# Constant matmuls on TensorE around the last norm of the first layer's batches, in a two-layer decoder kernel

## The chip, the cores and the metric

The kernel runs on one core of a Trainium2 chip, in one launch. The metric is the device time of that launch in microseconds. Engines are called by the profile's names: PE is TensorE's matmul, PEld its weight load, DVE is VectorE, ACT is ScalarE, POOL is GpSimd, and SP is SyncE, which only issues DMAs here.

## The reference, cut to what matters

The whole is a decoder of two layers on x of shape (4, 512, 256) in float32; each sublayer is added to the stream after a layer norm.

```python
x = x + _L0_attn_ref(_layernorm(x), ...)            # selective scan, then attention and a gated FFN
x = x + _L0_xattn_ref(_layernorm(x), ctx_1024, mask, ...)
x = x + _L0_ffn_ref(_layernorm(x), ...)             # 8 experts, top 1
x = x + _L1_attn_ref(_layernorm(x), ...)
x = x + _L1_xattn_ref(_layernorm(x), ctx_1024, ctx_1024, ...)
x = x + _L1_ffn_ref(_layernorm(x), ...)             # 16 experts, top C tokens, and a shared FFN

def _layernorm(x, axis=-1, eps=1e-05):
    m = jnp.mean(x, axis=axis, keepdims=True)
    v = jnp.var(x, axis=axis, keepdims=True)
    return (x - m) / jnp.sqrt(v + eps)

def step(h, inp):                                    # the selective scan, 512 steps, 512 channels, 16 states
    x_t, d_t, B_t, C_t = inp
    dA = jnp.exp(d_t[:, :, None] * A)
    h = dA * h + d_t[:, :, None] * B_t[:, None, :] * x_t[:, :, None]
    y_t = jnp.sum(h * C_t[:, None, :], axis=-1)
    return (h, y_t)
```

The change lies in the norm before the first layer's expert FFN, and reaches into the start of the next batch's scan.

## The kernel before, in words

The program is written out by hand: each engine has its own instruction stream, and semaphores order them. Activations are kept with features on the partitions, 2 x 128 features by the 512 tokens of one batch (`xb`, `xc`, `sq`, `xn`). PSUM has 8 banks of 512 float32 columns.

After a first part that computes the scan's inputs for all four batches comes the loop of L743, `for b in range(B)`, once per batch:

1. **The scan** (L795 to L809). For each of the 16 states PE makes the input term: `input_term(n)` (L774) multiplies four 128x128 blocks of `duT` for each of four channel groups with diagonal blocks that ACT wrote (`spread_b`, L1525, seen as L1530), into banks 4 to 7. DVE scans each bank against the decays that ACT exponentiated (L1523; the scans are L1963). POOL multiplies the scanned states with C (L2462), and PE adds the product to y (`add_to_y`, L787, seen as L791). `input_term(n + 2)` stands before the addition of state n, so PE's order is input term, addition, input term, addition.
2. The output projection (L815), attention, the gated FFN, and cross-attention, whose last product goes through L967 into banks 2 and 3. DVE adds it to `xb` (L1958).
3. **The end of the batch** (L971 to L988), where the change lies. PE makes the mean in bank 0 (two matmuls of 512 columns, seen as L642, which is the line of the helper `acc`). If there is a next batch, PE then makes that batch's first input term, `input_term(0, b + 1)`. DVE centres (L1806), ACT squares (L1431). `norm_var(3, 1)` puts the variance in bank 1, eight matmuls with one moving column each. ACT takes the root (L1435), DVE inverts it (L1810), and `norm_rows(3, 0)` spreads the factors over the 128 partitions in bank 0, four matmuls of 128 columns, seen as L660. DVE multiplies (L1815, `xn`). PE transposes `xn` (L983) into the tiles of group "xn" for ACT (L1638), which stores it for the routing, and makes the router's logits, matmuls of 8 columns (L642 again), in bank 3. DVE adds their bias (L2079).

DVE's stream at the end of a batch, in order: L1806, L1810, L1815, the scans of channel groups 0 and 1 of the next batch's state 0, the logits' addition (L2079), then the scans of groups 2 and 3 and on into the next batch's loop. ACT's stream there: squares, `spread_b(1)`, the root, the decays of state 0, the two drains of the transposes (L1638), then the loop of the next batch.

PE's next instructions after the logits are `input_term(1)` and `input_term(2)` of the next batch. `input_term(n)` waits, for each of the four channel groups, for the scan of that group in state n-1 (L781), since it overwrites its bank. After the fourth batch the routing of the expert FFN follows instead: it needs the logits on DVE, and PE has two small matmuls in it (L994, L995).

A float32 matmul appears in the trace as two records with two weight loads; a transpose appears as one record.

Of the kernel before, what the change touches and what calls it, by code (L numbers as in the profile page):

```python
# [6 lines left out]
B, L, D = 4, 512, 256  # L7
# [130 lines left out]
def decoder_program(nc, A, out):  # L138
# [5 lines left out]
    with ctx:  # L144
# [17 lines left out]
        def take(*shape, at=None):  # L162
            n = int(np.prod(shape))
            o = top[0] if at is None else at
            if at is None:
                top[0] += n
                assert top[0] <= WORDS, top[0]
            v = arena[:, o:o + n]
            if len(shape) == 2:
                v = v.rearrange("p (a b) -> p a b", a=shape[0])  # L170
            if len(shape) == 3:
                v = v.rearrange("p (a b c) -> p a b c", a=shape[0], b=shape[1])
            return v
# [15 lines left out]
        const = take(C_COLS)  # L189
        vec = take(V_COLS)  # L190
        ident = const[:, C_ID:C_ID + P]
# [155 lines left out]
        bank = [psum[:, i, :] for i in range(8)]  # L347
# [288 lines left out]
        def _(pe):  # L636
            mm, transpose = nc.tensor.matmul, nc.tensor.transpose

            def acc(dst, pairs):

                for i, (w, x) in enumerate(pairs):
                    r = mm(dst, w, x, start=i == 0, stop=i == len(pairs) - 1)  # L642
                return r
# [47 lines left out]
            for s in range(B + 2):  # L691
# [34 lines left out]
                if b1 < B:  # L726
                    for half, f, n in ((0, a_r0, 1), (1, a_r1, 5)):
# [3 lines left out]
                        for c in range(NC):  # L731
                            r = mm(bank[4 + half][:, c * P:(c + 1) * P], f[:, c:c + 1].broadcast_to([P, P]), ident,
                                   start=True, stop=True)
# [9 lines left out]
            for b in range(B):  # L743
                def w(s, n):
                    pe.wait_ge(s.sem, s.at(n, b))
# [28 lines left out]
                def input_term(n, b=b):  # L774

                    pe.wait_ge(diag_ready.sem, diag_ready.at(NC * (n + 1), b))
                    for c in range(KI):
                        if n == 0:
                            pe.wait_ge(ld_scan.sem, ld_scan.at(48, b))
                        else:  # L780
                            pe.wait_ge(scan_done.sem, scan_done.at(KI * (n - 1) + c + 1, b))  # L781
                        for q in range(NC):
                            r = mm(bank[4 + c][:, q * P:(q + 1) * P], duT[:, q, c * P:(c + 1) * P], diag[n % 2][:, q, :],  # L783
                                   start=True, stop=True)
                        r.then_inc(b_full.sem, 1)
# [186 lines left out]
                norm_mean(xb, 0)  # L972
                if b + 1 < B:
                    input_term(0, b + 1)
                norm_var(3, 1)
                norm_rows(3, 0)
                w(na.out, 4)
                for half in range(2):
                    t = LA.fill(pe, b, "xn", half)
# [47 lines left out]
            def w0(s, n):  # L1027
                pe.wait_ge(s.sem, s.at(n))
# [15 lines left out]
            def norm_var(i, squares, at):  # L1044
                w0(nb.sq, KD * (i + 1))
                for c in range(NC):
                    r = acc(bank[at][:, c:c + 1], [(squares[:, k, c * P:(c + 1) * P], mean1[:, 0:1]) for k in range(KD)])
                r.then_inc(nb.var.sem, 1)

            def norm_rows(i, factors, at):  # L1050
                w0(nb.rs, i + 1)
                for c in range(NC):
                    r = mm(bank[at][:, c * P:(c + 1) * P], factors[:, c:c + 1].broadcast_to([P, P]), ident, start=True, stop=True)
                r.then_inc(nb.rows.sem, 1)
# [343 lines left out]
            for n in range(E1):  # L1398
# [14 lines left out]
                for hf in range(2):  # L1413
                    for k in range(KH):
                        if hf == 0 and k >= KH - 3:
                            pe.wait_ge(he_ready.sem, he_ready.at(k + 1, n))
                        r = mm(bank[6 + hf][:, 0:D], h1[:, k, hf * P:(hf + 1) * P], wdb[j][:, k, :],  # L1417
                               start=k == 0, stop=k == KH - 1)
# [1224 lines left out]
```

## Time and profile before

| | |
|---|---|
| median of 3 runs | 2991.7 us |
| lowest, highest | 2984.35, 3001.02 us |
| the profiled execution's own time | 2999.19 us |
| its span, first to last instruction | 2997.4 us |
| mean granted clock of TensorE in it | 0.933 of full |
| PE busy | 2666.6 us (89%) |
| DVE, ACT, POOL busy | 1454.4, 1087.9, 682.0 us |

The span is what the trace shows from its first to its last instruction; 1.8 us of the execution's time lie outside it. An engine's busy time says how long it had work in flight, not that it set the pace: that is read stretch by stretch, from what ended its idle time. The granted clock is given as a fraction, 1.00 for 2.4 GHz and 0.50 for 1.2 GHz.

### The profile page before, as it was taken

The numbers are of one execution on the slowest core, as the hardware profiler recorded it, in microseconds if no ns is written. First come the engines' busy times: TensorE is split into PE (matmuls) and PEld (weight loads), VectorE is DVE, ScalarE is ACT, GpSimd is POOL, SyncE is SP. The second block draws the span as 40 slices with busy tenths as digits, with TensorE's granted clock in tenths as the row PEclk, the third lists the DMA queues.
The fourth block names the chain that finished last, engine by engine and source line by source line (L and its number), as shares of the span: only waits on it lengthen the run. The fifth ranks groups of instructions, "written<-read, shape, count | busy, mean of one in ns | idle before, by whom it ended". The sixth has DMA issues, their size and how long they took to land. (4 is left out here: it accounts for less than half of the span.)

```text
span 2997.4 us, 40191 instructions
## 1 busy us (share of the span) xinstructions
PE 2666.6 (89%) x16416; PEld 1578.4 (53%) x16417; DVE 1454.4 (49%) x2235; ACT 1087.9 (36%) x1885; POOL 682.0 (23%) x364
## 2 busy tenths in 40 slices
PE   7779999999999999999959968989989898699997
PEld 4355534754275435653248844353552543487876
DVE  5566346832875356732711135446444553644432
ACT  4673245622563255533412213443334433011111
POOL 0255034900763045701520020000000000022222
PEclk9889999999999999999969978999989998799999
DMA  5540002100030003100059820010100102044552
GB/s 194 211 169 22 0 1 110 44 1 0 1 138 15 1 1 117 37 0 1 8 204 328 327 68 8 8 30 8 22 22 1 22 8 88 16 151 148 171 166 63
DMA packets 62127, 219.26 MB, mean 73 GB/s; under 512 B 12293, under 2 KB 28122, under 8 KB 45178
## 3 DMA queue, kind: packets, MB, share of 16 engines
q1 hardware_dynamic: 45802, 187.39, 17.3%
q0 software_dynamic: 9568, 18.75, 2.5%
q10 hardware_dynamic: 6576, 10.57, 1.0%
q8 instruction: 130, 2.13, 0.3%
q14 instruction: 51, 0.42, 0.0%
HBM read 172.50 MB, written 39.99 MB: 71 GB/s over the span
## 5 line engine op out<-in xcount | busy, mean ns | idle before, releaser
L642 PE MATMUL psum<-arena 128*128 128x256 f32 (+7 forms) x4224 | 1108.2, 414 | 68.0 <-ACT arena L1500 11.5
L642 PEld LDWEIGHTS psum<-arena 128*128 128x128 f32 (+1 forms) x4224 | 687.3, 198 | 439.3 <-issue 325.9
L2462 POOL TENSOR_TENSOR arena<-arena 128x1024 f32<-128x1024 f32 x128 | 300.0, 2370 | 111.6 <-DVE arena L1963 96.6
L1963 DVE TENSOR_TENSOR_SCAN arena<-arena,psum 128x512 f32<-128x512 f32 x256 | 291.5, 1201 | 26.5 <-PE psum L783 18.4
L783 PEld LDWEIGHTS psum<-arena 128*128 128x128 f32 x2048 | 243.2, 198 | 47.6 <-ACT arena L1530 40.3
L783 PE MATMUL psum<-arena 128*128 128x128 f32 x2048 | 253.9, 284 | 1.9 <-issue 1.9
L2497 POOL DMA_INDIRECT arena<-xn,arena x32 | 31.6, 989 | 913.9 <-DVE arena L2404 862.6
L2469 POOL TENSOR_TENSOR arena<-arena 128x1024 f32<-128x1024 f32 x32 | 76.0, 2374 | 655.2 <-ACT arena L1618 655.2
L2057 DVE SCALAR_TENSOR_TENSOR arena<-psum,arena 128x1024 f32<-128x1024 f32 x128 | 156.9, 1245 | 80.5 <-PE psum L928 80.1
L1618 ACT ACTIVATE arena<-arena 128x1024 f32<-128x1024 f32 x128 | 147.1, 1149 | 109.9 <-DVE arena L2057 109.7
L1224 PE MATMUL psum<-arena 32*128 32x512 f32 x512 | 175.8, 681 | 3.1 <-DVE arena L2255 3.1
L1755 ACT ACTIVATE arena<-psum 128x1024 f32<-128x1024 f32 x128 | 125.1, 1023 | 112.1 <-PE psum L1246 112.1
L1795 ACT ACTIVATE arena<-psum 128x256 f32<-128x256 f32 x128 | 49.3, 385 | 318.9 <-PE psum L642 311.4
L1523 ACT ACTIVATE arena<-arena 128x512 f32<-128x512 f32 x256 | 163.4, 711 | 0.0
L2258 DVE TENSOR_REDUCE arena<-psum 128x1 f32<-128x512 f32 x192 | 123.9, 687 | 67.0 <-PE psum L1224 66.0
L2473 POOL TENSOR_TENSOR arena<-arena 128x1024 f32<-128x1024 f32 x64 | 151.3, 2364 | 10.1 <-ACT arena L1618 1.2
L939 PE MATMUL psum<-arena 128*64 128x512 f32 x512 | 138.2, 617 | 15.6 <-ACT arena L1618 7.4
L928 PE MATMUL psum<-arena 64*128 64x512 f32 x512 | 142.5, 638 | 2.8 <-ACT arena L1596 2.8
L2041 DVE RECIPROCAL arena<-arena 128x256 f32<-128x256 f32 x64 | 110.9, 1743 | 46.2 <-ACT arena L1610 46.2
L1246 PE MATMUL psum<-arena 32*128 32x512 f32 x512 | 126.3, 664 | 4.1 <-ACT arena L1755 4.1
L1417 PE MATMUL psum<-arena 128*128 128x256 f32 x512 | 117.7, 382 | 0.0
L1530 ACT ACTIVATE arena<-arena 128x128 f32<-128x128 f32 x256 | 82.0, 392 | 82.4 <-PE psum L783 59.8
(290 smaller groups left out, 2980.0 us busy)
## 6 DMA issues: line engine op xcount, KB each, us to landing
arena<-in_W SPq DMA_DIRECT2D x46, 1024.0 KB
arena<-c_rows SPq DMA_DIRECT2D x32, 512.0 KB, 3.8
arena<-in_Wg SPq DMA_DIRECT2D x16, 1024.0 KB
arena<-in_Wu SPq DMA_DIRECT2D x16, 1024.0 KB
arena<-in_Wd SPq DMA_DIRECT2D x16, 1024.0 KB
arena<-in_xT SPq DMA_DIRECT2D x8, 512.0 KB, 5.5
zs_all<-arena SPq DMA_DIRECT2D x4, 1024.0 KB, 3.9
ut_all<-arena SPq DMA_DIRECT2D x4, 1024.0 KB, 8.7
```

The source lines that it names most:

```text
L642: r = mm(dst, w, x, start=i == 0, stop=i == len(pairs) - 1)
L783: r = mm(bank[4 + c][:, q * P:(q + 1) * P], duT[:, q, c * P:(c + 1) * P], diag[n % 2][:, q, :], start=True, stop=True)
L928: i = mm(bank[2 + 2 * (u % SBUFS) + r], xkT[64 * r:64 * r + 64, hp, kc * P:(kc + 1) * P], xqT[64 * r:64 * r + 64, hp, :], start=True, stop ...
L939: i = mm(bank[0][64 * r:64 * r + 64, :], v1[:, kc, 2 * hp + r, :], t2[u % TBUFS][:, r, :], start=kc == 0, stop=kc == NC - 1)
L1224: mm(t, q4[32 * j:32 * j + 32, g, qc * P:(qc + 1) * P], k4[32 * j:32 * j + 32, g, :], start=True, stop=True).then_inc((s1_full if u < LH e ...
L1246: r = mm(bank[4 + 2 * (v % 2) + j % 2], k4[32 * j:32 * j + 32, g, kc * P:(kc + 1) * P], q4[32 * j:32 * j + 32, g, :], start=True, stop=True)
L1523: A_(dA[n % 2][:, c, :], dl[:, c, :], ACT.Exp, scale=aneg[:, c, n:n + 1]).then_inc(dA_ready.sem, 1)
L1618: A_(t2[u % TBUFS], rl[u % RBUFS], ACT.Square, scale=0.125, bias=vec[:, V_NB:V_NB + 1])\
L1963: V.tensor_tensor_scan(hs[n % 3][:, c, :], dA[n % 2][:, c, :], bank[4 + c], 0.0, ALU.mult, ALU.add)\
L2057: V.scalar_tensor_tensor(rl[u % RBUFS], t, minus_nb8, bound[:, kc, :].unsqueeze(1).broadcast_to([P, 2, L]), ALU.max, ALU.min).then_inc(rel ...
L2462: nc.gpsimd.tensor_tensor(h, h, c_all[:, n % CBUFS, :].unsqueeze(1).broadcast_to([P, 2, L]), ALU.mult)\
L2473: nc.gpsimd.tensor_tensor(t, t, t2[kc], ALU.add).then_inc(tsum_step.sem, 1)
```

## The change

After `norm_var(3, 1)` PE multiplies the identity with the first 512 columns of the constants into bank 3 once, and after `norm_rows(3, 0)` twice. Both operands stand in SBUF from the kernel's start, and the matmuls wait for nothing and signal nothing. Bank 3 held a tile of the cross-attention's output, which DVE has added by then (`dve_has("xo", 2)`, L971); nobody reads it again before the logits, which PE itself writes over it afterwards, in its own order. All four batches get the three matmuls. Nothing else is changed, removed or moved on any other engine or queue.

```diff
@@ -972,8 +972,14 @@
                 norm_mean(xb, 0)
                 if b + 1 < B:
                     input_term(0, b + 1)
+                def turn_over(times):
+                    for _ in range(times):
+                        mm(bank[3], ident, const[:, 0:L], start=True, stop=True)
+
                 norm_var(3, 1)
+                turn_over(1)
                 norm_rows(3, 0)
+                turn_over(2)
                 w(na.out, 4)
                 for half in range(2):
                     t = LA.fill(pe, b, "xn", half)
```

PE's instructions at the end of the first batch, before the change. L783 of 16 is the next batch's first input term, L642 with one column the variance, L660 the rows, L983 the transposes, L642 with 8 columns the logits, and L783 of 32 the input terms 1 and 2 (a matmul counts once here):

```order
L642 MATMUL psum<-arena 128x512 x2
L783 MATMUL psum<-arena 128x128 x16
L642 MATMUL psum<-arena 128x1 x8
L660 MATMUL psum<-arena 128x128 x4
L983 MATMUL psum<-arena 128x128 x8
L642 MATMUL psum<-arena 128x8 x8
L783 MATMUL psum<-arena 128x128 x32
L791 MATMUL psum<-arena 32x512 x32
```

The same place with the change, where the transposes are line 989:

```order
L642 MATMUL psum<-arena 128x512 x2
L783 MATMUL psum<-arena 128x128 x16
L642 MATMUL psum<-arena 128x1 x8
L977 MATMUL psum<-arena 128x512
L660 MATMUL psum<-arena 128x128 x4
L977 MATMUL psum<-arena 128x512 x2
L989 MATMUL psum<-arena 128x128 x8
L642 MATMUL psum<-arena 128x8 x8
L783 MATMUL psum<-arena 128x128 x32
L791 MATMUL psum<-arena 32x512 x32
```

The new matmuls (L977) stand between what was there; the order of the rest is the same.

At the end of the fourth batch, where no input term stands between mean and variance and none follows the logits, the difference on PE is this:

```order
 L642 MATMUL psum<-arena 128x512 x2
 L642 MATMUL psum<-arena 128x1 x8
+L977 MATMUL psum<-arena 128x512
 L660 MATMUL psum<-arena 128x128 x4
-L983 MATMUL psum<-arena 128x128 x8
+L977 MATMUL psum<-arena 128x512 x2
+L989 MATMUL psum<-arena 128x128 x8
 L642 MATMUL psum<-arena 128x8 x8
```

Here too three matmuls are put in and the rest keeps its place.

## Rows read from the trace of the kernel before

**Rows 1.** The page: PE's busy time, and its granted clock in 40 slices.
```profile
PE 2666.6 (89%) x16416; PEld 1578.4 (53%) x16417; DVE 1454.4 (49%) x2235; ACT 1087.9 (36%) x1885; POOL 682.0 (23%) x364
...
PEclk9889999999999999999969978999989998799999
```

**Rows 2.** Timeline, end of the first batch: start us, us, engine, line, what [idle before <-releaser].
```profile
494.50 7.04 PE L967 MATMUL psum<-arena 128*128 128x512 f32 x16
...
502.32 1.99 PE L642 MATMUL psum<-arena 128*128 128x512 f32 x4 [0.78 <-DVE arena L1958]
...
507.72 1.84 PE L642 MATMUL psum<-arena 128*128 128x1 f32 x16
...
510.13 2.08 PE L660 MATMUL psum<-arena 128*128 128x128 f32 x8 [0.57 <-DVE arena L1810]
...
512.24 1.22 DVE L1815 TENSOR_TENSOR arena<-arena,psum 128x1024 f32<-128x1024 f32 x1 [2.17 <-PE psum L660]
513.38 2.33 DVE L1963 TENSOR_TENSOR_SCAN arena<-arena,psum 128x512 f32<-128x512 f32 x2
...
513.52 1.97 PE L983 MATMUL psum<-arena 128*128 128x128 f32 x8 [1.31 <-DVE arena L1815]
...
515.28 3.42 PE L642 MATMUL psum<-arena 128*128 128x8 f32 x16
...
518.55 9.89 PE L783 MATMUL psum<-arena 128*128 128x128 f32 x64
...
518.84 4.79 DVE L1963 TENSOR_TENSOR_SCAN arena<-arena,psum 128x512 f32<-128x512 f32 x4
...
524.08 6.78 DVE L1963 TENSOR_TENSOR_SCAN arena<-arena,psum 128x512 f32<-128x512 f32 x6 [0.45 <-PE psum L783]
...
528.37 2.35 PE L791 MATMUL psum<-arena 32*32 32x512 f32 x64
...
530.65 3.84 PE L783 MATMUL psum<-arena 128*128 128x128 f32 x32
```

**Rows 3.** Windows there: us, busy (instructions) of PE, PEld, DVE, ACT, POOL, PEclk, DMA, GB/s.
```profile
507.50:510.00 2.50, 2.06 (x20) 1.97 (x18) 0.11 (x1) 0.39 (x2) 0.00 (x0) 1.00 1.00 413
510.00:513.50 3.50, 2.08 (x8) 1.78 (x8) 1.33 (x3) 3.49 (x5) 0.00 (x0) 0.52 0.79 314
513.50:518.50 5.00, 4.98 (x24) 4.99 (x25) 2.20 (x2) 3.82 (x8) 2.35 (x1) 0.50 0.28 93
518.50:523.50 5.00, 5.00 (x24) 5.00 (x25) 4.62 (x5) 3.70 (x9) 2.19 (x1) 0.50 0.39 120
523.50:528.50 5.00, 5.00 (x59) 4.88 (x74) 4.55 (x5) 3.59 (x8) 4.46 (x3) 0.97 0.00 0
```

**Rows 4.** Windows at the same place of the second and the third batch.
```profile
841.20:844.70 3.50, 2.08 (x8) 1.78 (x8) 1.33 (x3) 3.49 (x5) 0.00 (x0) 0.51 0.78 309
...
1172.30:1175.80 3.50, 2.07 (x8) 1.78 (x8) 1.33 (x3) 3.49 (x5) 0.00 (x0) 0.51 0.80 314
```

**Rows 5.** Timeline of PE at the end of the fourth batch.
```profile
1499.81 3.42 PE L642 MATMUL psum<-arena 128*128 128x1 f32 x16 [2.04 <-ACT arena L1431]
...
1503.79 2.08 PE L660 MATMUL psum<-arena 128*128 128x128 f32 x8 [0.57 <-DVE arena L1810]
...
1507.18 1.97 PE L983 MATMUL psum<-arena 128*128 128x128 f32 x8 [1.31 <-DVE arena L1815]
...
1508.94 3.42 PE L642 MATMUL psum<-arena 128*128 128x8 f32 x16
```

**Rows 6.** Timeline of POOL in the scan's even stretch, two states.
```profile
539.29 9.51 POOL L2462 TENSOR_TENSOR arena<-arena 128x1024 f32<-128x1024 f32 x4 [0.17 <-DVE arena L1963]
```

**Rows 7.** Windows: the output projection after a wait; the second batch's second norm among matmuls.
```profile
599.00:605.70 6.70, 5.70 (x7) 2.52 (x8) 2.05 (x4) 0.00 (x0) 0.00 (x0) 0.50 0.00 0
...
672.00:683.00 11.00, 11.00 (x45) 6.38 (x44) 3.67 (x7) 3.98 (x5) 0.00 (x0) 1.00 0.00 0
```

**Rows 8.** Timeline of PE: the rows of that second norm.
```profile
681.87 1.05 PE L660 MATMUL psum<-arena 128*128 128x128 f32 x8
```

## The prediction

> **What bounds the kernel now.** I read the page first: PE is busy for 89% of the span, and its granted clock is below full in many slices [rows 1]. So time comes from PE's waits and from stretches at the lower clock. I then read the timeline around the edited lines, with all engines, and cut the same stretch into windows to see the clock. Last I looked up the other batches, the norms that lie among matmuls, and the pace of the scan behind the change.
>
> At the end of the first batch PE works without a break until 501.5, waits 0.78 us, makes the mean and the next batch's first input term, and then the variance: 16 records of one column in 1.84 us [rows 2]. The clock is 1.00 up to 510.00 and 0.50 soon after [rows 3]. What PE did before it fell is two matmuls with 512 columns, the input term until 507.7, and then 1.84 us of one-column records and a wait of 0.57 [rows 2]. It did not stop for long anywhere: no wait in this stretch is over 1.31 us [rows 2]. From there the rows, the transposes, the logits and half of two input terms run at 0.50, until about 523.8, where the window's mean is 0.97 again [rows 3]. The second and the third batch show the same fall in the same place [rows 4]. After the fourth batch the variance already takes 3.42 us for 16 records, so it runs at half clock too [rows 5].
>
> Is this stretch on the path? PE's chain behind the logits is without a gap: logits to 518.55, the input terms 1 and 2 for 9.89 us, the first additions at 528.37, the third input term at 530.65, and so on [rows 2]. In the even stretch two states take 9.51 + 0.17 = 9.68 us, 4.84 us per state [rows 6], which is PE's 3.84 for an input term and the rest for its addition: PE sets the pace, and POOL, with 4.76 us of work per state, has 0.08 to spare. So what PE wins before 528.37 should be kept to the end of the scan. DVE is close behind: its scans wait for the logits' addition and start at 518.84 [rows 2].
>
> **What the change adds.** Per batch three matmuls of 512 columns, six records. At full clock 16 such records take 7.04 us and 4 take 1.99, so one more takes (7.04 - 1.99) / 12 = 0.42 [rows 2]: 0.85 us for a pair of records, 1.7 for two pairs. At half clock 7 records take 5.70 us, 0.81 each [rows 7], and twice 0.42 is 0.84; I take 1.7 for a pair and 3.4 for two. Nothing is removed or moved, and no DMA or queue is touched.
>
> **What it should do at the first three places.** All hangs on whether the clock stays up. The nearest rows for it are the same norm operations where other matmuls of 512 columns lie between them: variance and rows of the second norm run in a window at 1.00, and the rows take 1.05 us there instead of 2.08 [rows 7, 8]. The change copies that pattern: something wide after the variance, something wide after the rows. The first pair begins at about 509.5, ahead of the fall at 510.1. So I take the clock as kept, and follow PE:
> - The variance ends at 509.56. The first pair runs to about 510.4, so the rows start 0.3 us later than 510.13.
> - The rows take 1.05 instead of 2.08: they end at 511.5 instead of 512.2, and DVE's multiply starts 0.7 us earlier and ends at 512.8.
> - The second and third pair follow the rows' last issue, 511.4, and end at 513.1. So they hold up the transposes by 0.3 us, and these start at 513.1 instead of 513.52: 0.4 won.
> - The eight transposes keep PE 0.12 us each as input-term records do (3.84 / 32 [rows 2]), 0.96 instead of 1.76 (513.52 to 515.28): 0.8 won.
> - The logits' 16 narrow records take what the variance's 16 take at full clock, 1.84 instead of 3.27 (515.28 to 518.55): 1.4 won. PE comes to the input terms at 515.9, and DVE to its next scan at about 516.2 instead of 518.84: 2.6 won.
> - The two input terms need 7.7 us at full clock instead of 9.8, by PE alone to 523.6. But the last group of the second waits for the sixth of DVE's scans from 516.2; six at 1.2 (4.79 / 4 [rows 2]) end at 523.4, and the group's 0.96 makes 524.4. The additions start at 524.4 instead of 528.37: **3.9 us per place**, of which DVE's pace withholds about 0.8.
>
> POOL could withhold more: its second product of state 0 can start at about 518.7, and at 9.51 / 4 = 2.38 each [rows 6] the fifth after it, with which state 3 begins, can start at 530.6. By PE's pace the third input term starts at 530.65 - 3.9 = 526.7, and DVE has scanned its first two groups at 526.7 + 0.96 + 2 x 1.2 = 530.1. So POOL withholds 0.5 us of that product at most, and I count nothing for it. Three places give 11.7 us.
>
> **What it should do at the fourth.** Here the clock has fallen before the first added matmul can act, while PE waited 2.04 us for ACT's squares [rows 5]. The first pair takes 1.7 from 1503.2, so the rows start at 1504.9, 1.15 late. If the clock stays low, the other pairs end at 1504.9 + 1.76 + 3.4 = 1510.1, and the transposes are 2.9 us late. If the unbroken work brings it back by the end of the rows, the pairs end at 1508.4 and transposes and logits, 0.96 + 1.84, at 1511.2 instead of 1512.4: 1.2 won. Neither is excluded; I take 0 and keep both ends. No gain beyond that is possible, since the routing behind it is DVE's and DMA's.
>
> **Sum.** The profiled execution took 2999.19 us, so it would take 2987.5. It lies 7.5 above the median of the runs shown, 2991.7. A run that was faster may have lost less at these places, so I take 11 off the median: **2981 us**, 0.36% less. A measurement of this kernel can tell about 0.5%, 15 us, from no change.
>
> **A rule that speaks against it.** By the rows the clock fell although no wait there is over 1.31 us [rows 2, 3]. The Trainium skill (TensorE: Matmul & The Clock Gate, Why this matters for your kernels) warns of long idle gaps of PE between bursts of matmuls; by that rule read alone the clock would not fall here, and filling these short gaps would be worth nothing. The rows disagree with it. The same page (Part 4: PE-mode transpose) says that transposes do not count as PE being busy in the way matmuls do. No row here separates the two; by that rule the first rival below would be the outcome.
>
> **Rivals.**
> - *The fall comes later.* The pairs carry the clock over the rows, but the transposes and the eight-column logits, 2.8 us, are like the variance's one-column records, and it falls in them. Then only the 0.4 us before the transposes is won at each place, and up to 2 us where it falls after the logits. Three places at 0.4: 2990.5. For it: the stretch is longer than the variance's. Against it: 1.7 us of wide matmuls lie right before and an input term right behind. 0.14.
> - *The clock falls anyway, and the added matmuls run at half clock.* It decides at 510.1, whether the pair, which begins at 509.5, comes in time. Then the rows start at 509.6 + 1.7 = 511.3, 1.2 late, and the transposes at 511.3 + 1.76 + 3.4 = 516.5, 3.0 late, as at the fourth place. DVE's scans and PE's input terms follow them. Four places at 3.0: 2991.7 + 12 = 3003.7, slower. For it: only about half a microsecond of the pair lies before the fall. Against it: the same pattern at the keys. 0.08.
> - *The gain is made and does not arrive.* The scan's start is earlier, but POOL, with 0.08 us per state to spare, or a late load of `ut` or `zs` sets its end. Half of 11 would be left: 2986. 0.08.
> - *More than forecast.* Where the fall is avoided at all four places (1.2 more at the fourth) and the 11 moves later falls to a kinder spot, 15 to 20 us: 2974. This is the forecast's own upper end, counted in it.
>
> **How the numbers follow.** Forecast 0.70, late fall 0.14, lower clock 0.08, lost gain 0.08. Of the forecast's 0.70 I put 0.29 above 15 us, for its size may be 9 to 15 and the runs shown spread by 17 us from lowest to highest; the rest and both mild rivals are within 0.5%. The slower rival is at 0.4%, so about half of it passes the bound. Faster 0.29, same 0.66, slower 0.05. The range takes 15 us of gain and 10 of spread below, and the late fall with some spread above: 2967 to 2995.
>
> **What would show it.** Right: windows at the three places with a clock of 1.00 from 507 to 528; rows of L660 near 1.05 us there; L977 records 0.42 us apart; 16 logit records in 1.84; from the mean's start to the first additions 22.1 us instead of 26.05. Wrong: a clock of 0.50 anywhere in there, L977 records 0.84 apart, a transpose that waits for no engine but starts later than 11.2 us after the mean; or a scan whose states take over 4.84 us after an early start.

## The result, and the profile after

The change takes 2981.52 us at the median of nine runs (2970.17 to 2983.68), the kernel before 2992.22 us (2984.35 to 3002.3). The ratio is 0.9945, with a 95% interval of 0.9928 to 0.9962: 0.55% faster, and forecast were 2981 us and 0.36%. A second measurement, beside other kernels (run f1 below), gave 0.9959 with 0.9943 to 0.9975. The profiled execution took 2970.17 us, the fastest of the nine, for a span of 2968.3 us. The profiled execution of the kernel before took 2999.19 us, well above its median of 2992.22. So the 29 us between the two profiled executions are not the size of the change, and I compare stretch by stretch.

The page of the kernel after, PE's busy time and its granted clock:

```profile
PE 2648.8 (89%) x16440; PEld 1563.7 (53%) x16441; DVE 1453.5 (49%) x2235; ACT 1084.1 (37%) x1885; POOL 681.2 (23%) x364
...
PEclk9879999999999999999979977999999998799999
```

PE's busy time went down by 18 us, though 24 records were added: the other records take less time at the higher clock. The slices are too coarse to show more.

The timeline of the first batch's end after the change, with the columns of [rows 2]:

```profile
501.54 1.99 PE L642 MATMUL psum<-arena 128*128 128x512 f32 x4 [0.78 <-DVE arena L1964]
...
506.93 1.84 PE L642 MATMUL psum<-arena 128*128 128x1 f32 x16
...
508.64 1.10 PE L977 MATMUL psum<-arena 128*128 128x512 f32 x2
...
509.58 1.05 PE L660 MATMUL psum<-arena 128*128 128x128 f32 x8
...
510.47 1.88 PE L977 MATMUL psum<-arena 128*128 128x512 f32 x4
...
512.19 1.04 PE L989 MATMUL psum<-arena 128*128 128x128 f32 x8
...
513.06 1.85 PE L642 MATMUL psum<-arena 128*128 128x8 f32 x16
...
514.77 8.27 PE L783 MATMUL psum<-arena 128*128 128x128 f32 x64
...
515.06 11.21 DVE L1969 TENSOR_TENSOR_SCAN arena<-arena,psum 128x512 f32<-128x512 f32 x10
...
522.97 2.35 PE L791 MATMUL psum<-arena 32*32 32x512 f32 x64
```

The windows over it:

```profile
507.00:509.50 2.50, 2.50 (x19) 2.07 (x19) 0.18 (x1) 0.67 (x2) 0.00 (x0) 1.00 1.00 406
509.50:512.50 3.00, 3.00 (x16) 1.94 (x16) 1.83 (x2) 2.99 (x5) 0.00 (x0) 1.00 0.76 298
512.50:515.00 2.50, 2.50 (x25) 2.50 (x24) 1.68 (x3) 2.50 (x5) 0.70 (x1) 1.00 0.04 15
515.00:519.00 4.00, 3.96 (x35) 3.79 (x35) 4.00 (x5) 4.00 (x10) 3.15 (x2) 1.00 0.80 253
```

The clock is 1.00 where it was 0.50 in [rows 3], and the rows (L660) take 1.05 us instead of 2.08. From the start of the mean to the first additions the stretch takes 522.97 - 501.54 = 21.43 us, against 528.37 - 502.32 = 26.05 before. This stretch is the measure of nearly all that follows, and I call it **the stretch**. The second batch's end is the same (849.31 - 827.88 = 21.43), and the third too; before they were 25.99 and 25.98.

```profile
827.88 1.99 PE L642 MATMUL psum<-arena 128*128 128x512 f32 x4 [0.78 <-DVE arena L1964]
...
849.31 1.14 PE L791 MATMUL psum<-arena 32*32 32x512 f32 x32
```

Behind it nothing is given back. PE's timeline at the end of the second batch's scan, after the change (first two lines) and before it (last line):

```profile
591.84 1.15 PE L791 MATMUL psum<-arena 32*32 32x512 f32 x32 [2.39 <-POOL arena L2468]
594.60 9.76 PE L815 MATMUL psum<-arena 128*128 128x512 f32 x16 [1.61 <-DVE arena L1985]
...
600.00 9.95 PE L815 MATMUL psum<-arena 128*128 128x512 f32 x16 [1.60 <-DVE arena L1979]
```

From the first additions to the output projection (L815) it takes 594.60 - 522.97 = 71.63 us, and before 600.00 - 528.37 = 71.63. Behind the other two places it is the same to 0.01 us. The fourth batch's end after the change, to be read beside [rows 5]:

```profile
1479.77 1.99 PE L642 MATMUL psum<-arena 128*128 128x512 f32 x4 [0.78 <-DVE arena L1964]
1483.80 3.43 PE L642 MATMUL psum<-arena 128*128 128x1 f32 x16 [2.04 <-ACT arena L1437]
1487.10 2.05 PE L977 MATMUL psum<-arena 128*128 128x512 f32 x2
1488.94 1.92 PE L660 MATMUL psum<-arena 128*128 128x128 f32 x8
1490.65 1.97 PE L977 MATMUL psum<-arena 128*128 128x512 f32 x4
1492.45 1.04 PE L989 MATMUL psum<-arena 128*128 128x128 f32 x8
1493.33 1.85 PE L642 MATMUL psum<-arena 128*128 128x8 f32 x16
1497.55 0.22 PE L1000 MATMUL psum<-arena 128*128 128x128 bf16 x1 [2.37 <-DVE arena L2102]
```

The variance and the rows are still at half clock, transposes and logits no longer. From the mean's start to the first routing matmul it takes 17.78 us; before it was 18.95 (1495.78 to 1514.73):

```profile
1495.78 1.99 PE L642 MATMUL psum<-arena 128*128 128x512 f32 x4 [0.78 <-DVE arena L1958]
...
1514.73 0.27 PE L994 MATMUL psum<-arena 128*128 128x128 bf16 x1 [2.37 <-DVE arena L2096]
```

So the edit gives 4.62 + 4.56 + 4.55 + 1.17 = 14.9 us in this pair of profiles. Up to the routing matmul the whole difference is 1514.73 - 1497.55 = 17.2 us. The other 2.3 lie in code that the change does not touch: 0.8 ahead of the first place, and 1.5 between the projections and the means. Behind the routing matmul the profiles differ by another 11.9 us (1482.7 us to the end of the span against 1470.8). Over all thirteen profiles of this study that unchanged rest takes 1469.7 to 1488.7 us, and the change's own second profile has 1483.6. That is scatter from execution to execution, as large as the change itself.

### The profile page after: what moved, and what is told of

It reads as the page before. It is cut to its first block and busy times, and to the rows that moved or that the text cites. A ratio compares the mean times of both kernels' runs of the same rounds, so it can differ in the third digit from the quotient of the medians.

```text
span 2968.3 us, 40239 instructions
## 1 busy us (share of the span) xinstructions
PE 2648.8 (89%) x16440; PEld 1563.7 (53%) x16441; DVE 1453.5 (49%) x2235; ACT 1084.1 (37%) x1885; POOL 681.2 (23%) x364
## 5 line engine op out<-in xcount | busy, mean ns | idle before, releaser
L642 PE MATMUL psum<-arena 128*128 128x256 f32 (+7 forms) x4224 | 1096.6, 411 | 65.0 <-ACT arena L1506 11.5
L642 PEld LDWEIGHTS psum<-arena 128*128 128x128 f32 (+1 forms) x4224 | 680.3, 197 | 430.7 <-issue 317.2
L1969 DVE TENSOR_TENSOR_SCAN arena<-arena,psum 128x512 f32<-128x512 f32 x256 | 290.9, 1201 | 22.4 <-PE psum L783 14.5
L783 PEld LDWEIGHTS psum<-arena 128*128 128x128 f32 x2048 | 236.7, 193 | 49.2 <-ACT arena L1536 40.3
L783 PE MATMUL psum<-arena 128*128 128x128 f32 x2048 | 249.0, 279 | 2.0 <-issue 1.9
L2433 DVE TENSOR_TENSOR arena<-arena,psum 128x256 f32<-128x256 f32 x128 | 53.2, 421 | 115.3 <-ACT arena L1801 113.2
```

Of the source, the lines that this page charges most:

```text
L1969: V.tensor_tensor_scan(hs[n % 3][:, c, :], dA[n % 2][:, c, :], bank[4 + c], 0.0, ALU.mult, ALU.add)\
```

## Experiments

All keep the change's two positions, after `norm_var(3, 1)` and after `norm_rows(3, 0)`, unless said otherwise.

**One position alone.** e1 keeps the first and drops the second, e2 the reverse:

```diff
 e1                        |  e2
 norm_var(3, 1)            |  norm_var(3, 1)
 turn_over(1)              | -turn_over(1)
 norm_rows(3, 0)           |  norm_rows(3, 0)
-turn_over(2)              |  turn_over(2)
```

> One matmul after the variance, none after the rows. Measured at the first three batch ends, from the start of the mean to the first additions to y: 26.0 us in the kernel before, 21.4 with the change. Theory (the clock falls when PE has moved few columns for a while): the fall at the variance is gone, but the wait after the rows is bare, so the clock falls later at some of the places, during the transposes or logits: between 21.3 and 23.6 us, not the same at all runs. Rival (only the stretch at the variance matters): 21.3 at every place. Rival (the gain is from both together, and each alone is too little): near 26.

Measured for e1: 2981.79 us, ratio 0.9945 (0.9925 to 0.9965), the same as the change. The stretch took 21.25, 22.00 and 21.24 us. At the second place the clock fell, but later than before, at about 844.5, as the logits ended (844.46). The windows there:

```profile
838.00:844.00 6.00, 4.68 (x36) 4.01 (x37) 3.64 (x4) 5.29 (x9) 0.00 (x0) 1.00 0.63 251
844.00:848.00 4.00, 4.00 (x23) 4.00 (x23) 3.37 (x5) 4.00 (x10) 3.15 (x2) 0.57 0.79 254
848.00:852.00 4.00, 4.00 (x38) 4.00 (x38) 3.96 (x5) 3.92 (x10) 3.99 (x3) 1.00 0.04 12
```

It is low in most of the window from 844 to 848, is back after it, and the stretch is 0.75 us longer. The forecast's rival of a late fall is therefore real, but it occurred in a kernel without the second position, and it costs less than I had given it: the clock fell only behind the logits and was back, with the input terms on PE, at about 848. At the two places without a fall e1 is 0.18 us quicker than the change, since its transposes do not stand behind two matmuls.

> Two matmuls after the rows, none after the variance. Same stretch, 26.0 before, 21.4 with the change. Theory: the one-column variance and the wait behind it are bare, so the clock may fall there at 509 to 513 us as before, but the matmuls behind the rows bring it back sooner: 21.3 to 23.0 us, the fall lasting fewer microseconds than the 13.7 of before. Rival (the fall, once there, lasts as it did, and two matmuls at half clock delay the transposes by 1.7 us): 27 to 28 us, slower than before.

Measured for e2: 2985.2 us, ratio 0.9960 (0.9938 to 0.9983), stretches of 22.93, 22.83 and 22.83. Its windows at the first place:

```profile
507.00:510.40 3.40, 2.94 (x28) 2.86 (x26) 0.12 (x1) 1.25 (x5) 0.00 (x0) 1.00 1.00 413
510.50:513.90 3.40, 3.39 (x10) 2.54 (x11) 1.28 (x2) 3.39 (x5) 0.00 (x0) 0.50 0.77 305
514.00:518.00 4.00, 4.00 (x32) 3.47 (x31) 2.47 (x4) 2.63 (x6) 1.75 (x1) 1.00 0.11 40
```

Here the clock falls where it fell before, and with the two wide matmuls behind the rows it is back by 514, not 523.8. They run mostly at half clock (2.47 us to the next instruction, 1.72 in the change) and delay the transposes to 12.1 us behind the mean (11.2 before), and still the stretch is 3.1 to 3.2 us shorter. So a fall is not dear by itself; its length is. Each position alone brings two thirds of the 4.6 us or more, by different ways: the first prevents the fall, the second ends it early.

**What the matmuls must be.** e3 replaces every 512-column matmul by four matmuls of one column, e4 by seven transposes:

```diff
-mm(bank[3], ident, const[:, 0:L], start=True, stop=True)
+for _ in range(4):                                                   # e3
+    mm(bank[3][:, 0:1], ident, const[:, 0:1], start=True, stop=True)
+for q in range(7):                                                   # e4
+    transpose(bank[3][:, 0:P], const[:, (q % 4) * P:(q % 4 + 1) * P], ident)
```

> The same two positions, but each 512-column matmul is replaced by four matmuls with one moving column, eight records, about 0.9 us: PE is as busy and waits as little, but moves almost no columns. Theory (columns count): the clock falls as before at all three places, and the added records are at half clock after the fall: the stretch takes 26 us or up to 2 more. Rival (it is PE's idle gaps that count, and the change closes them): clock at 1.00 throughout and 21.4 us.

e3 took 3003.19 us, ratio 1.0024 (1.0003 to 1.0046): slower than the kernel before, if barely clear of it. The stretches were 25.50, 25.50 and 27.12 us, 78.1 in sum and 78.0 before. So the gain is gone, but the stretches do not explain why the whole is slower still; that stays open. At the first place, timeline and windows:

```profile
508.72 1.03 PE L978 MATMUL psum<-arena 128*128 128x1 f32 x8
...
510.59 2.76 PE L978 MATMUL psum<-arena 128*128 128x1 f32 x16
```

```profile
507.00:511.00 4.00, 4.00 (x39) 4.00 (x37) 0.39 (x2) 2.08 (x3) 0.00 (x0) 1.00 1.01 406
511.00:515.00 4.00, 4.00 (x22) 4.00 (x23) 3.25 (x3) 2.63 (x5) 0.58 (x1) 0.54 0.24 98
515.00:521.00 6.00, 6.00 (x30) 6.00 (x30) 2.60 (x4) 5.81 (x12) 1.80 (x2) 0.50 0.55 177
```

PE is busy for 4.00 of 4.00 us up to 511, there is no idle gap at all, and the clock falls all the same at about 511.3. At the other two places it falls too, at about 842.4 and 1170.1, and again PE has no idle time between the input term and the fall. So filling PE's time is not enough; these one-column matmuls did not hold the clock. Closed idle gaps alone as the cause of the change's gain are refuted. The Trainium skill's advice to avoid long idle gaps (TensorE: Matmul & The Clock Gate, Why this matters for your kernels) is not wrong by this, but here gaps do not tell where the clock falls.

> The same two positions, but each 512-column matmul is replaced by seven transposes of 128x128 blocks of the constants, about 0.85 us at full clock. Theory A (transposes count for the clock like matmuls of as many columns): the clock stays at 1.00 and the stretch takes 21.4 us. Theory B (the Trainium skill, TensorE: Matmul & The Clock Gate, Part 4: transposes do not count as PE being busy in the same way): the clock falls as before, and the stretch takes 26 to 28 us.

e4 took 2976.81 us, ratio 0.9926 (0.9899 to 0.9953), with stretches of 21.11 us at all three places:

```profile
512.40 1.69 PE L978 MATMUL psum<-arena 128*128 128x128 f32 x14
...
513.93 1.04 PE L990 MATMUL psum<-arena 128*128 128x128 f32 x8
```

```profile
507.00:511.00 4.00, 4.00 (x39) 4.00 (x38) 0.00 (x0) 1.87 (x7) 0.00 (x0) 1.00 1.00 417
511.00:515.00 4.00, 4.00 (x40) 3.98 (x37) 2.58 (x4) 3.97 (x7) 0.00 (x0) 1.00 0.73 290
515.00:523.00 8.00, 7.95 (x67) 7.57 (x68) 7.37 (x8) 8.00 (x19) 6.11 (x3) 1.00 0.41 133
```

Transposes of full blocks held the clock here as the wide matmuls did, and are a little shorter (the 14 behind the rows took 1.53 us to the next instruction, the four matmul records 1.72). The Trainium skill says in the same page, Part 4: PE-mode transpose, that transposes do not count in that way; for these float32 transposes the runs show otherwise, and the measurement decides.

**Where it acts, and what too much costs.**

```diff
-turn_over(1)                          # e5
+turn_over(1 if b + 1 < B else 0)
-turn_over(2)
+turn_over(2 if b + 1 < B else 0)
```

> The added matmuls only at the ends of the first three batches. There, from the mean's start to the first additions: 21.4 us as with the change. At the fourth end, from the mean's start to the first routing matmul: 18.95 us before, 17.8 in the change's profile. Theory (the fourth place gains when its matmuls bring the clock back before the transposes): without them 18.2 to 19.0 us. Rival (they only delay there): under 17.8.

A single execution of e5 took 2975.13 us, with stretches of 21.43 at the three places. The fourth end took 17.48 us, outside the theory's figures and inside the rival's. The expectation had been made for a variance at half clock. In this execution it ran at full:

```profile
1487.14 1.95 PE L642 MATMUL psum<-arena 128*128 128x1 f32 x16 [2.04 <-ACT arena L1437]
...
1494.80 3.42 PE L642 MATMUL psum<-arena 128*128 128x8 f32 x16
```

The fourth end must be compared among like executions. With the variance at half clock: 18.95 without the added matmuls, 17.78 with them. With the variance at full clock: 17.48 without, 16.13 with them (e7 below). So the three matmuls are worth 1.2 to 1.35 us there either way, by one or two executions each; whether the variance is at full clock is worth 1.5 to 1.65 more, and no added matmul of this batch end lies ahead of it. But fewer do better at this end: with the variance at half clock e2, without the matmul behind the variance, took 17.27 us where the change took 17.78, and with it at full clock e1, without the two behind the rows, took 15.62 where e7 took 16.13. Three are more than the fourth end needs.

e6 doubles the change to two matmuls and four:

```diff
-turn_over(1)
+turn_over(2)
 norm_rows(3, 0)
-turn_over(2)
+turn_over(4)
```

> Two matmuls after the variance and four after the rows, twice the change. The clock is up already, so the rest is only cost: the rows start 0.85 us later, and the transposes another 1.7. Theory: from the mean's start to the transposes 13.2 us (10.65 with the change, 11.2 before), to the first additions 24.0 (21.4 and 26.0). If the added matmuls were hidden even then: 21.4. Clock at 1.00 at all three places.

A single execution took 2984.04 us. The transposes start 13.23 us behind the mean, the stretch is 24.00 at all three places, the fourth end 18.74. What was added beyond the change is paid in full (2.57 us per place).

```profile
517.31 1.04 PE L989 MATMUL psum<-arena 128*128 128x128 f32 x8
```

**The same means elsewhere.** The clock also falls at the scan's end [rows 7], where PE waits for POOL and then for DVE. e7 adds to the change:

```diff
+                    if n == NS - 1:
+                        w(scan_done, KI * (NS - 1) + 1)
+                        turn_over(4 if b == 0 else 2, 4)
                     w(hc_ready, 4 * (n + 1))
...
+                turn_over(2, 4)
                 w(yz_ready, 2)
```

Here `turn_over` has the bank as its second argument; bank 4 is free once DVE has scanned channel group 0 of the last state.

> The change, and also at the end of every scan: two matmuls of 512 columns (four in the first batch) into bank 4 before the last addition, where PE waits for POOL, and two behind it, where it waits for DVE. Before and with the change the clock falls there, at 598.9 in the profile before, and the output projection runs at half clock for most of its 9.95 us. Theory (columns moved in the waits keep the clock): the projection takes 7.0 us, 3 less in each of four batches, and the start is not later by more than 0.2: some 12 us less than the change, 2969 us. Rival (the waits are too long or the additions too thin, the clock falls all the same): the matmuls then run at half clock and delay the projection by up to 1.8 us: 2981 to 2988.

e7 took 2972.77 us, ratio 0.9934 (0.9914 to 0.9955). The mechanism is as expected, at all four scans:

```profile
588.60 1.15 PE L795 MATMUL psum<-arena 32*32 32x512 f32 x32 [0.47 <-POOL arena L2472]
589.68 1.98 PE L757 MATMUL psum<-arena 128*128 128x512 f32 x4
...
591.50 7.04 PE L823 MATMUL psum<-arena 128*128 128x512 f32 x16
```

The projection (L823 there) takes 7.04 us in every batch, where the change's profile has 8.53, 9.76, 8.73 and 9.85, and the way to it is only 0.14 us longer (93.20 us from the mean, 93.06 with the change). The size is not as expected. From the projection's start to the next mean the four batches took 230.6, 232.2, 233.6 and 232.3 us, with the change 232.2, 233.3, 232.4 and 233.4. So of 2.2 us per batch that the projection wins on average, only 0.6 is left at the next mean: the rest is given back where the clock falls in later places. Between the projections and the next means, windows of 0.5 us show 13.7 us at the lower clock in the change's profile, over the four batches, and 27.3 us in e7's (27.2 when e7 was run again, f2 below). The third batch's timeline of e7 shows one such fall, where the scores begin and PE waits for ACT:

```profile
941.39 0.49 PE L852 MATMUL psum<-arena 64*128 64x128 f32 x2 [0.69 <-ACT arena L1561]
...
943.57 0.79 PE L852 MATMUL psum<-arena 64*128 64x128 f32 x2
...
944.59 4.05 PE L642 MATMUL psum<-arena 128*128 128x64 f32 x6
```

The same L852 records take 0.49 us for two before the fall and 0.79 behind it, and 0.48 at the same point of the third batch in the change's profile (L844 there, at 949.19), where the clock is still up. Why the clock falls at more places once it has been kept at the scan's end is not shown.

> As the run with the scan's end filled, and at the fourth batch's end two matmuls of 512 columns more, between mean and variance, where PE waits 2.04 us for ACT's squares. Theory: the variance there takes 1.84 us instead of 3.42 and the clock stays up to the logits: from the mean's start to the first routing matmul 15.2 to 15.9 us (18.95 before, 17.8 with the change), so about 2 us less than the run with the scan's end alone: 2967 us. Rival (the fall at the fourth place comes from elsewhere): 17.8 again.

e8 adds `turn_over(2)` between mean and variance of the fourth batch. It took 2977.02 us, ratio 0.9947 (0.9930 to 0.9964), and its fourth end 16.14 us, just what e7 has (16.13). Neither side of the expectation holds. In both runs the variance was at full clock already, at 1.95 us for its 16 records, and the clock fell during the matmul behind it (1.58 and 1.59 us for two records, 1.10 at full clock, 2.05 at half); two more matmuls ahead of the variance did not prevent that. The time is that of the change, although e8 holds all of e7, so the scan's end shows no gain by this run.

**The comparison on one chip.**

> The change itself once more, beside the two that follow, on one chip. From the mean's start to the first additions 21.4 us at the first three batch ends; time 2977 to 2984 us, 0.3 to 0.7% under the kernel before.

> The run with the scan's end filled as well, against the change on the same chip. The projection took 7.04 us instead of 9.8, but the stretch from the projection to the next mean gave only part of it back: 230.6 to 233.6 us, 232.2 to 233.4 with the change. Theory (about half of the 12 us is kept, since later thin spots let the clock fall again): 4 to 6 us less than the change. Rival (all is given back): the same as the change.

> As the run with the scan's end filled, with one matmul instead of two after the rows. Theory (one is enough to keep the clock, and the second holds the transposes up by 0.24 us, as the run without any showed): from the mean's start to the transposes 10.4 us, to the first additions 21.25, at the first three ends, with the clock at 1.00 there. If one is too little, one or more of the places shows 22 to 23.6. In the whole time 0.5 us at most, not to be told.

| kernel | median us | ratio to before, 95% interval | stretch at three places | fourth end |
|---|---|---|---|---|
| the change (f1) | 2979.04 | 0.9959, 0.9943 to 0.9975 | 21.43, 21.43, 21.43 | 17.77 |
| e7 again (f2) | 2968.26 | 0.9925, 0.9907 to 0.9942 | 21.43, 21.43, 21.43 | 16.14 |
| e9 | 2971.03 | 0.9929, 0.9913 to 0.9944 | 21.25, 21.25, 22.00 | 15.58 |

f1 met its expectation. f2 is 10.8 us below the change, more than the 4 to 6 expected; the two intervals just fail to meet. The two profiled executions are 14.2 us apart: 6.6 us are there by the routing matmul (1491.07 against 1497.67), and the rest lies in the unchanged part behind it, whose scatter is known from above. So beside each other on one chip the version with the scan's end filled beats the change. In the earlier measurements it did not clearly (e7's interval overlaps the change's, and e8 came out level with it), and how much comes from the projections stays open. e9 has one matmul after the rows instead of two. Its transposes start 10.41 us behind the mean, as expected, but at the third place the clock fell once behind the logits, and that took 0.75 back. That is one fall in three places, as in e1 with none behind the rows; so one isn't shown to be better than none. With two behind the rows and one behind the variance all 18 places in six profiles took 21.42 to 21.44 us (the change, f1, e5, e7, f2, e8). The second costs 0.18 us and is the safe choice, as in the change.

## Why the prediction was right

**The mechanism.** The text took the clock as kept because the same norm runs at full clock among the keys' matmuls. It was, at all three places in the change's two profiles. e3, with about as much PE time in one-column matmuls at the same positions, lost the clock, so the gain is not that of a busier PE; e1 and e2 show that each position has its own part.

**The terms.** The rows took 1.05 us as forecast. The added records came 0.43 apart (1.72 us from 510.47 to 512.19 for four), forecast 0.42. The transposes started 10.65 us behind the mean; forecast 513.1 - 502.32 = 10.8. The transposes kept PE 0.87 us instead of 0.96, the logits 1.71 instead of 1.84: I had taken the length of a group of rows, which has its last record's own length in it, for its step to the next one. And DVE's scans go at 1.12 us each when PE keeps up (11.21 for 10), not at the 1.2 that the half-clock stretch showed; [rows 2] has 6.78 us for six behind that stretch, 1.13 each, so the better figure was at hand. These are why the stretch gained 4.6 and not 3.9: PE came to the input terms 3.0 us earlier and not 2.6, and from there to the additions it took 8.20 us and not 8.5. POOL withheld nothing: the third and the fourth input term come 4.84 us apart (525.25 and 530.09), the even pace of before, and neither they nor the additions wait for POOL.

```profile
525.25 3.84 PE L783 MATMUL psum<-arena 128*128 128x128 f32 x32
529.01 1.14 PE L791 MATMUL psum<-arena 32*32 32x512 f32 x32
```

**The fourth place** was left at 0 between a loss of 2.9 and a gain of 1.2. The gain came, 1.17, by the way described for it: the clock came back by the end of the rows, before the second pair (1.97 us for its four records, 1.88 at full clock). That the clock has fallen by the variance there, which the text took as given, holds for some executions only: in e1, e3, e5 and e6, and wherever the scan's end was filled, the variance ran at full clock.

**The sum.** 14.9 us by the profiles against 11.7 in the text, and 0.55% or 0.41% by the two measurements against 0.36%. The median hit 2981 within 0.5 us, and that is luck: the stretches gained 3 us more than forecast, the two medians lie only 10.7 us apart (14.5 in the second measurement), and the unchanged rest alone scatters by 19 us. The mechanism and its terms are what was right. The text also took 0.5% as the least that a measurement can tell from no change; the interval came out at 0.17% either way. Of the rivals, the late fall happened only in kernels with fewer matmuls (e1, e9) and cost 0.75 us where it did. The half-clock rival did not occur at the first three places: the matmul behind the variance came in time in every profile that had it with 512 columns. The gain arrived whole, as 71.63 us on both sides show. The rule on idle gaps and the rule on transposes, both weighed ahead, are answered by e3 and e4.

## What to carry to other kernels

Where a stretch on the critical path ends with narrow matmuls and short waits, look at the granted clock in windows of a few microseconds before looking at the waits: here the slow clock cost 4.6 of 26 us although no wait of PE was longer than 1.31. Wide matmuls or full-block transposes into an unread bank held the clock here, and at little cost where they fit into waits that exist; one-column matmuls did not, and what went beyond the waits was paid in full (e6). Measure the stretch itself, since a kernel of this length scatters by more than the gain, and expect the next thin place to take some of it back.

## What the runs showed of the hardware that was not expected

- A fall of the clock came without any idle time of PE: in e3 PE was busy for 4.00 of 4.00 us before it (window 507 to 511) and the clock went to 0.50, the lower of its two levels, 1.2 GHz.
- Float32 transposes of 128x128 blocks held the clock at 1.00, 2.4 GHz, as matmuls of 512 columns did (e4).
- A fall was cut short: with two 512-column matmuls behind the rows the clock was back at about 514 in e2, and without them, in the kernel before, it stayed at half until 523.8.
- With the clock kept at the scan's end it was low for longer behind it: 27.3 us (e7) and 27.2 (f2) between projections and means, 13.7 with the change.
- The unchanged second half of the kernel took between 1469.7 and 1488.7 us in thirteen profiles.
